# A two-layer graph attention kernel: head norms taken along rows with Newton steps on GpSimd, and a second layer norm taken by row chunks

## The reference

```python
# layer 0: 4 heads of 64
q, k, v = h @ Wq, h @ Wk, h @ Wv
attn = softmax(where(adj, q k^T * scale, -max));  out = (attn @ v) @ Wo + bo
# layer 1: 8 heads of 64
m = embs @ map_w.T + map_b
norm = max(||m_head||, 1e-8);  n = m_head / norm          # per node and head
cos_adj = (n n^T * ~mask > 0.1)
q, k = m @ q_w.T + q_b, m @ k_w.T + k_b
p = softmax(where(mask, -1e10, q k^T / 8)) * keep
adj_h = cos_adj * p
out = relu((adj_h @ sem_h) @ gcn_W.T / (adj_h.sum(-1) + 1))
```

## Time and profile before

| | us |
|---|---|
| median of 3 runs | 4123.62 |
| lowest, highest | 4120.02, 4124.43 |
| the profiled execution | 4121.26 |
| its span, first to last instruction | 4119.5 |
| TensorE busy | 3931.4 (95%) |
| TensorE weight loads busy | 3437.0 (83%) |
| VectorE busy | 2608.3 (63%) |
| ScalarE busy | 1979.3 (48%) |
| GpSimd busy | 1324.3 (32%) |

### The profile page before, as it was taken

One profiled execution on the slowest core, in us unless ns is written; L12 is line 12 of the kernel. 1 busy time (PEld: TensorE's weight loads), 2 busy tenths in 40 slices (PEclk: granted clock), 3 DMA queues, 4 the chain that ended last, 5 costly groups with the idle time before them and its releaser, 6 DMA issues.

```text
span 4119.5 us, 105002 instructions
## 1 busy us (share of the span) xinstructions
PE 3931.4 (95%) x32976; PEld 3437.0 (83%) x32976; DVE 2608.3 (63%) x9426; ACT 1979.3 (48%) x5583; POOL 1324.3 (32%) x2007
## 2 busy tenths in 40 slices
PE   7999999999999999999999999999999999999997
PEld 6888888888888888888888888888888888888886
DVE  4666666666666666666666666666666666666664
ACT  3554544544545445445454454454454544544544
POOL 3333333333332333333333333333333333333332
PEclk8999999999999999999999999999999999999998
DMA  3000000000000000000000000000000000000000
GB/s 87 16 32 26 22 32 16 32 32 16 32 27 21 32 18 30 32 16 32 29 18 32 22 25 32 16 32 32 16 32 27 21 32 16 32 32 16 32 27 17
DMA packets 65544, 111.77 MB, mean 27 GB/s; under 512 B 20880, under 2 KB 22448, under 8 KB 65520
## 3 DMA queue, kind: packets, MB, share of 16 engines
q1 hardware_dynamic: 64928, 110.12, 7.8%
q0 software_dynamic: 592, 1.35, 0.2%
HBM read 44.34 MB, written 33.55 MB: 19 GB/s over the span
## 4 chain that ended last, share of the span: by engine, by line
PE 65%; DVE 12%; issue 11%; ACT 6%; POOL 4%; DVEq 1%; DMA 1%; POOLq 0%; ACTq 0%; SPq 0%
PE bank L755 34%; PE bank L763 9%; PE bank L748 7%; PE bank L783 6%; PE bank L775 4%; ACT prob L501 3%; PE bank L883 3%; POOL prob L417 2%; DVE x_mid L663 2%; ACT att L475 2%; DVE prob L650 2%; DVE att L607 2%; DVE att L618 1%; POOL rstd L362 1%; DVE hT L640 1%
## 5 line engine op out<-in xcount | busy, mean ns | idle before, releaser
L475 ACT ACTIVATE att<-att,nmax 128x256 f32<-128x256 f32 x1024 | 509.7, 500 | 299.6 <-DVE nmax L607 299.6
L417 POOL TENSOR_SCALAR prob<-prob,rsum 128x256 f32<-128x256 f32 x512 | 241.1, 487 | 631.2 <-DVE rsum L657 628.2
L755 PE MATMUL bank<-hT,w_qkv 128*128 128x256 f32 x3072 | 414.9, 288 | 4.7 <-DVE hT L640 4.7
L755 PE MATMUL bank<-qkm,w_k 128*128 128x256 f32 x3072 | 416.6, 285 | 0.0
L755 PEld LDWEIGHTS bank<-hT,w_qkv 128*128 128x128 f32 x3072 | 376.9, 189 | 37.9 <-issue 24.2
L755 PE MATMUL bank<-hT,w_map 128*128 128x256 f32 x3072 | 396.7, 285 | 5.1 <-DVE hT L640 1.0
L618 DVE SCALAR_TENSOR_TENSOR att<-bank,att 128x256 f32<-128x256 f32 x1024 | 392.3, 420 | 4.0
L755 PE MATMUL bank<-qkm,w_q 128*128 128x256 f32 x3072 | 390.8, 283 | 0.0
L755 PEld LDWEIGHTS bank<-hT,w_map 128*128 128x128 f32 x3072 | 372.5, 189 | 18.4 <-DVE hT L640 17.3
L763 PE MATMUL bank<-w_v,hT 128*128 128x512 f32 x1536 | 385.3, 399 | 0.0
L755 PEld LDWEIGHTS bank<-qkm,w_k 128*128 128x128 f32 x3072 | 380.1, 188 | 5.0
(11 more groups left out here) (122 smaller groups left out, 7949.6 us busy)
## 6 DMA issues: line engine op xcount, KB each, us to landing
x_in<-x SPq DMA_DIRECT2D x64, 512.0 KB, 3.4
x_res<-x_mid SPq DMA_DIRECT2D x64, 512.0 KB, 3.1
out<-x_res SPq DMA_DIRECT2D x64, 512.0 KB, 2.8
adj<-adj SPq DMA_DIRECT2D x64, 64.0 KB, 2.6
att<-gcn_map POOLq DMA_DIRECT2D x2, 512.0 KB, 9.0
x_mid<-wq SPq DMA_DIRECT2D x1, 512.0 KB, 5.6
x_res<-wk SPq DMA_DIRECT2D x1, 512.0 KB, 6.8
v<-wv SPq DMA_DIRECT2D x1, 512.0 KB, 7.7
```

The costliest lines, as they stand in the source:

```text
L417: last = g.tensor_scalar(prob0[:, hd, c, :], prob0[:, hd, c, :], rsum0[:, hd, c:c + 1], 0.0, ALU.mult, ALU.add)
L475: s_.activation(e_sl, e_sl, ACT.Exp, bias=nmax1[:, p, c, e:e + 1], scale=-1.0, accum_out=esum1[:, p, c, e:e + 1]).then_inc(exp1_done, 1)
L755: last = t_.matmul(dst, w(ws, k)[:, t * 128:t * 128 + 128], rhs[:, rs, k, :], start=(k == 0 and i == 0), stop=(k == KT - 1 and i == 2))
```

## The change

Four things change together, and all five lists are new in order.

- Head norms as rows. GpSimd still squares `m32`. ScalarE rounds pairs of squares to fp32r (`sq0`, `sq1`) into the space of `nrm`, GpSimd subtracts to get the rest (`lo0`, `lo1`, 128x512 each). `ss` becomes 8 matmuls of 256 columns with a 0/1 selector `sel` as weights, whose output is already `[40, 256]`: rows 0 to 7 and again rows 32 to 39. The `rt` transposes on TensorE go.
- Inverse root by Newton steps. VectorE clamps and makes a first guess by an integer trick; GpSimd does three steps of four operations each on `[40, 256]`, each waiting for the one before; VectorE's `rt` then makes `rnT`.
- Layer norm by chunks. Each row chunk has its own aggregate, `rstd` and `norm`. `ht?a` and `ht?b` are now row chunks, and `qk*` and `m*` wait for `ht?b`.
- PSUM. `score` has banks 0 and 1 for itself and `cos` has 2 and 3, so both can be issued ahead of the turns. `turn_a`, `turn_b`, `value` and `back` share bank 4, one after the other. Products go round banks 5 to 7 (`PBANKS = 3`).

Its core (start-up code, waits in `SYNC`, and declarations are cut):

```diff
     TENSOR = [
-        "ht0a", ("score", 0), "ht0b", ("cos", 0), "qk0", "qk1", ("turn_a", 0), "qk2", ("turn_b", 0), "s0", "s1", ("value", 0),
-        "qk3", ("back", 0), ("score", 1), ("cos", 1), "s2", "s3", "pt0", "v0", "pt1", ("turn_a", 1), ("turn_b", 1), "pt2",
-        "pt3", ("value", 1), "av", ("back", 1), ("score", 2), ("cos", 2), "wo0", "wo1", ("turn_a", 2), ("turn_b", 2),
-        ("value", 2), ("score", 3), ("back", 2), "ht1a", "ht1b", ("cos", 3), "m0", "m1", "m2", ("turn_a", 3), ("turn_b", 3),
-        "m3", ("value", 3), "vv0", "ss", "q2", "q1", "q0", "k1", ("back", 3), "rt", "k0", "q3", "k3", "bc0", "bc1", "k2",
-        "vv1"
+        ("score", 0), "ht0a", "ht0b", ("cos", 0), ("score", 1), "qk0", "qk1", ("turn_a", 0), "qk2", ("turn_b", 0), "qk3",
+        ("value", 0), "s0", "s1", ("cos", 1), ("score", 2), "s2", "s3", ("back", 0), "v0", ("turn_a", 1), "pt0", "pt1",
+        ("turn_b", 1), "pt2", "pt3", ("value", 1), "av", ("back", 1), ("cos", 2), "wo0", "wo1", ("turn_a", 2), ("score", 3),
+        ("cos", 3), ("turn_b", 2), "ht1a", "ht1b", ("value", 2), "m0", ("back", 2), "m1", ("turn_a", 3), "m2", ("turn_b", 3),
+        "m3", ("value", 3), "vv0", "q1", "ss", "q2", "q0", "k0", "q3", "k2", ("back", 3), "k3", "vv1", "bc0", "k1", "bc1"
     ]
     SCALAR = [
...
+        ("exp_a", 1), ("exp_b", 1), ("unit", 1), ("value", 0), "exp0", "exp1", "exp2", "exp3", ("turn_a", 1), "pt0", "pt1",
+        ("turn_b", 1), "pt2", "pt3", ("exp_a", 2), ("value", 1), ("exp_b", 2), "av", ("turn_a", 2), ("turn_b", 2), "ht1a",
+        "ht1b", ("value", 2), ("exp_a", 3), "m0", ("exp_b", 3), "m1", ("turn_a", 3), "m2", ("turn_b", 3), "sq0", "m3", "sq1",
+        "q1", "q2", "q0", ("value", 3), "k0", "q3", "k3", "k2", "k1"
     VECTOR = [
...
+        "wo0", "wo1", "norm1a", "norm1b", ("score_a", 3), "ht1a", "ht1b", ("score_b", 3), ("cos_a", 3), ("factor", 2),
+        ("back", 2), ("cos_b", 3), "m0", "m1", "m2", "m3", "stats0", "vv0", "norm0", "q1", "ss", ("factor", 3), "q2", "q0",
+        "k0", "q3", "rt", "k2", "k3", ("back", 3), "vv1", "bc0", "bc1", "k1"
     POOL = [
-        ("unit", 0), "mid", "mask0", "sum0", "sum1", ("unit", 1), ("back", 0), "sum2", "sum3", "rstd1", ("back", 1),
-        ("back", 2), "m0", "rstd0", "m1", "m2", "m3", "pow", "mask1", ("back", 3)
+        ("unit", 0), "mask0", "mid", ("unit", 1), "sum0", ("back", 0), "sum1", "sum2", "sum3", ("back", 1), "rstd1a", "rstd1b",
+        "m0", "m1", "lo0", "m2", ("back", 2), "m3", "lo1", "rstd0", "root0", "root1", "root2", ("back", 3), "mask1"
     ]
-    PBANKS = 4
+    PBANKS = 3
...
+                    elif kind in ("root0", "root1", "root2"):
+                        k = 4 * (ROOT_STEPS * n + int(kind[4]))
+                        if kind == "root0":
+                            pool.wait_ge(guessed, n + 1)
...
+                        g.tensor_tensor(root_t, root_x, root_y, ALU.mult).then_inc(root_steps, 1)
+                        pool.wait_ge(root_steps, k + 1)
+                        pool.sem_inc(passed_gpsimd, 1)
+                        g.tensor_tensor(root_t, root_t, root_y, ALU.mult).then_inc(root_steps, 1)
+                        pool.wait_ge(root_steps, k + 2)
+                        pool.sem_inc(passed_gpsimd, 1)
+                        g.tensor_scalar(root_t, root_t, -0.5, 1.5, ALU.mult, ALU.add).then_inc(root_steps, 1)
+                        pool.wait_ge(root_steps, k + 3)
+                        pool.sem_inc(passed_gpsimd, 1)
+                        g.tensor_tensor(root_y, root_y, root_t, ALU.mult).then_inc(root_steps, 1)
...
                     elif kind == "ss":
-                        pe.wait_ge(msq_done, KT * n + KT)
+                        pe.wait_ge(sq_high_done, 2 * n + 2)
+                        pe.wait_ge(sq_low_done, 2 * n + 2)
                         empty(n, kind)
                         for t in range(KT):
-                            for c in range(C):
-                                last = t_.matmul(full[:, c * H1 + 2 * t:c * H1 + 2 * t + 2], msq[:, t, c * 128:c * 128 + 128], half_of[:, :], start=True, stop=True)
-                        last.then_inc(product_full, 1)
-                    elif kind == "rt":
-                        pe.wait_ge(rn_done, n + 1)
-                        empty(n, kind)
-                        for c in range(C):
-                            last = t_.transpose(full[0:H1, c * 128:c * 128 + 128], rn[:, c * H1:c * H1 + H1], ident[:, :])
+                            for i, part in enumerate((sq_high, sq_low)):
+                                last = t_.matmul(full[:, 0:N], sel[:, t, :], part[:, t, :], start=(t == 0 and i == 0), stop=(t == KT - 1 and i == 1))
                         last.then_inc(product_full, 1)
```

More of the change, by code:

```diff
@@ L19 @@
 COS_THRESHOLD = 0.1
+ROOT_GUESS = 1597463007.0
+ROOT_STEPS = 3
 MASKED_L1 = -1e10
@@ L61, in gnn_two_layers @@
-        ("turn_a", 1), ("turn_b", 1), "pt2", "pt3", ("value", 1), "av", ("exp_a", 2), ("exp_b", 2), ("turn_a", 2),
-        ("turn_b", 2), ("value", 2), "ht1a", "ht1b", ("exp_a", 3), "m0", ("exp_b", 3), "m1", ("turn_a", 3), "m2",
-        ("turn_b", 3), "m3", "q2", ("value", 3), "q1", "k1", "q0", "k0", "q3", "k3", "k2"
+        ("unit", 0), "ht0a", "ht0b", ("exp_a", 0), ("exp_b", 0), "qk0", "qk1", ("turn_a", 0), "qk2", ("turn_b", 0), "qk3",
+        ("exp_a", 1), ("exp_b", 1), ("unit", 1), ("value", 0), "exp0", "exp1", "exp2", "exp3", ("turn_a", 1), "pt0", "pt1",
@@ L192, in gnn_two_layers @@
         pick_made = count("pick_made")
+        sel_made = count("sel_made")
         fold_full = count("fold_full")
@@ L353, in _, with rstd_of @@
             pool.sem_inc(nlow_done, 2)
-            def rstd_of(k):
-                pool.wait_ge(stat_done, 4 * k + 4)
+            def rstd_of(k, c):
+                pool.wait_ge(stat_done, 4 * k + 2 * c + 2)
                 pool.sem_inc(passed_gpsimd, 1)
-                g.tensor_scalar(var_e[:, :], mv[:, :, 1], 1.0, LN_EPS, ALU.mult, ALU.add).then_inc(var_done, 1)
-                pool.wait_ge(var_done, 2 * k + 1)
+                g.tensor_scalar(var_e[:, c:c + 1], mv[:, c, 1:2], 1.0, LN_EPS, ALU.mult, ALU.add).then_inc(var_done, 1)
+                pool.wait_ge(var_done, 4 * k + 2 * c + 1)
                 pool.sem_inc(passed_gpsimd, 1)
-                g.tensor_tensor(rstd[:, :], var_e[:, :], minus_half[:, 0:C], ALU.pow).then_inc(var_done, 1)
-            pool.wait_ge(made, 9)
-            rstd_of(0)
+                g.tensor_tensor(rstd[:, c:c + 1], var_e[:, c:c + 1], minus_half[:, c:c + 1], ALU.pow).then_inc(var_done, 1)
+            pool.wait_ge(made, 15)
+            for c in range(C):
+                rstd_of(0, c)
             with nc.allow_non_contiguous_dma("small biases, once"):
@@ L672, in body @@
                                                 ALU.add, ALU.subtract).then_inc(product_done, 1)
-                    elif kind == "norm1":
-                        normalise(2 * n + 1, x_mid)
+                    elif kind in ("norm1a", "norm1b"):
+                        normalise(2 * n + 1, x_mid, "ab".index(kind[5]))
                     elif kind == "norm0":
-                        normalise(2 * n + 2, x_in)
+                        for c in range(C):
+                            normalise(2 * n + 2, x_in, c)
                     elif kind == "stats0":
                         dve.wait_ge(x_loaded, 16 * n + 32)
-                        row_stats(x_in, 0)
-                        row_stats(x_in, 1)
-                        mean_var(2 * n + 2)
+                        for c in range(C):
+                            row_stats(2 * n + 2, x_in, c)
                     elif kind in ("vv0", "vv1"):
@@ L822, in body @@
                     elif kind[:2] == "ht":
-                        t = 2 * "ab".index(kind[3])
-                        pe.wait_ge(h_ready, 4 * n + (2 if kind[2] == "0" else 4))
+                        c = "ab".index(kind[3])
+                        pe.wait_ge(h_ready, 4 * n + (1 if kind[2] == "0" else 3) + c)
                         empty(n, kind)
-                        transposes(full, lambda k, c: h[:, c, (t + k) * 128:(t + k + 1) * 128]).then_inc(product_full, 1)
+                        transposes(full, lambda k, half: h[:, c, (2 * k + half) * 128:(2 * k + half) * 128 + 128]).then_inc(product_full, 1)
                     elif kind[:2] == "qk":
@@ L829, in body @@
                         empty(n, kind)
-                        for chunks in (range(2), range(2, 4)):
-                            pe.wait_ge(product_done, out_of_psum(n, "ht0a" if chunks[0] == 0 else "ht0b"))
-                            last = project(full[:, 0:N], lambda s2, k: w_qkv[:, s2, w, k, :], t, hT, chunks)
-                        last.then_inc(product_full, 1)
+                        pe.wait_ge(product_done, out_of_psum(n, "ht0b"))
+                        project(full[:, 0:N], lambda s2, k: w_qkv[:, s2, w, k, :], t, hT).then_inc(product_full, 1)
                     elif kind == "v0":
@@ L864, in body @@
```

(6 more changed lines are left out.)

136 lines of the change are left out of this document (79 added, 57 removed), and 3 rows, old and new, of the table VECTOR.

## The result

The changed kernel takes 4222.6 us (4219.98 to 4223.51), the kernel before on the same chip 4124.0: 1.024 times as long, 95% interval 1.0222 to 1.0257. It is slower by 98.6 us, where +17 was forecast.

A forecast was written before the change was run, and what follows sets the result against it. TensorE, busy 95% of the span, was taken as the bound: its work plus holes. Terms summed to +0.32 us a round, times 63 +20, with the ends +17, added to 4123.6: 4141 us, range 4044 to 4200.

The forecast's parts named there:

- Work saved on TensorE: TensorE's work: `ss` as 8 matmuls and no `rt` transposes, -0.87 us a round.
- Second layer norm: TensorE's holes from `wo1` to `m0` shrink to 1.58 us from 2.75: -1.17 us a round.
- `pt3`: TensorE's hole at `pt3`, a wait for GpSimd's scaled `prob`, shrinks to 0.15 us: -0.18 a round.
- `q0`: TensorE waits at `q0` for the bank of `q1`, drained late behind `norm0`: +0.67 us a round.
- `bc0`: TensorE waits at `bc0` for the Newton chain, `rt` and the drain of `k2`: +0.72 us a round.
- Newton is longer: Rival on the GpSimd chain: a multiplication costs 0.74 us, the chain grows by 0.9, all uncovered: 4198 us, chance 0.17.
- Newton fits: Rival: holes at `q0`, `bc0` and `k1` (1.54 us) go in part or whole: 4044 to 4086 us, chance 0.33.
- `k1`: TensorE waits at `k1` for the bank of `k3`, which VectorE drains after `k2`: +0.15 us a round.
- `cos` 0: TensorE waits at `cos` 0 for `unit` 0, by way of ScalarE and GpSimd: +0.40 us a round.
- `wo0`: TensorE waits at the output projection, ScalarE's copy of `av` standing behind `exp_b` 2: +0.60 us a round.
- The ends: Outside the repeated rounds: start-up fills +2 us, first round +1, last round about -6.
- Rival B: Rival from the follow-ups: three product banks instead of four, and shared bank 4, hold TensorE up everywhere; two steps about 4205 us.

The follow-up runs named there:

- the run with four moves: Changed kernel with `norm0` behind `ss`, `rt` behind `k2` and `k3`, `av` ahead of `exp_b` 2, `score_a` 3 behind `ht1b`: 4087.6 us.
- two moves in one list: Changed kernel with, in VectorE's list, `norm0` behind `ss` and `rt` behind `k2` and `k3` but ahead of `back` 3: 4088.8 us, 0.9915 of before.

## Why the prediction was wrong, point by point

The measured 4222.6 lies above the range, which ended at 4200. The direction was the likeliest one, the size six times too small: 98.6 us for 17, from +1.41 a round instead of +0.32, and 18 us of a lower clock that had no term.

- **Work saved on TensorE** (-0.87): right. `ss` 0.94 instead of 0.97, and `rt` gone: -0.90.
- **Second layer norm** (-1.17): right in kind, too large. `m0` started 9.36 us behind `wo0`, where the walk gave 9.0 and the kernel before 10.18 (its 10.46 less the 0.28 that the walk leaves for `back` 2): -0.82. The time was lost on VectorE ahead of `ht1b`: its two aggregates wait for their statistics, for which the walk had no term, and the second ends at 5.32 on the round's clock instead of 4.9. From `ht1b` to `m0` it took 2.07, as walked (2.1). The hole ahead of `m0` was put on the mask ahead of `ht1a`; the run with four moves shows it is ScalarE's copy. The two aggregates, timeline of VectorE:

```profile
2068.28 0.18 DVE L574 BATCH_NORM_AGGREGATE mv<-stats 128x2 f32<-128x6 f32 x1 [0.15 <-DVE stats L571]
2070.05 0.18 DVE L574 BATCH_NORM_AGGREGATE mv<-stats 128x2 f32<-128x6 f32 x1 [0.15 <-DVE stats L571]
```

- **`pt3`** (-0.18): wrong, 0.38 before and after the change, now at `pt1`: 0.
- **`q0`** (+0.67): 0.38. Right place and releaser, shown by the run with `norm0` late.
- **`bc0`** (+0.72): 1.94. This is the term that failed, and all parts of it the same way. Newton's last operation ended at 35.03 of the round's clock instead of 34.4: 0.63, though the first started as walked (25.17 for 25.2). The multiplications took 0.73, not 0.64, nine times, +0.81, the scale-and-add 0.40, not 0.49, three times, -0.27, and the eleven hand-overs 0.1 more in all. I had bounded a multiplication by 0.62 and 0.74 and chosen half of a 512-wide operation. The error is in the halving: from 0.73 for 256 and 1.288 for 512 elements an operation costs 0.17 us once and 2.18 ns an element (an estimate from two points), and half of the long one drops half of the fixed part. The row of the same size and two different inputs, L410 with 738 ns, was right to 0.01 us; the 0.62 is of one tensor with itself. Then `rt` and the drain took 1.46 instead of 1.1 (0.28, 0.15 between, 0.41 and a drain of 0.48), and TensorE was ready at 34.55, not 34.8. 0.63 + 0.36 + 0.25 is 1.24, the size of the miss.
- The rival "Newton is longer" had just this price, 0.74, and this place, and gave 4198, still 24 us short. With 0.17 it was weighed too low: the chain had no slack, so each bound of its unknown cost was as near as the value I took. The rival "Newton fits", 4044 to 4086, is what the run with two steps shows, at 4062.4.
- **`k1`** (+0.15): 0.14. **`cos` 0** (+0.40): about 0.4, released by GpSimd's `nrm`, as forecast. **`wo0`** (+0.60): 0.3, and not by `exp_b` 2.
- Together the measured terms give +1.44, for 1.41 of the rounds. Without `bc0` the others miss by +0.35, +0.18, -0.29 and -0.30 and nearly cancel, which is luck.
- **The lower clock**: no case of the prediction had it. The first and last slices of the profile before showed it only where TensorE idles for long, and an idle time of 1.35 in each round was harmless there. Idle times of 1.8 and more weren't always, and the layer norm alone shows that none of that length is needed. It is 18 of the 98.6 us; with four steps each round has it.
- **The ends**: forecast -3, measured about -2 (4.2 + 1.9 - 8.3).
- What I hadn't seen at all is that the order of two names in VectorE's list could be worth 0.7 us through GpSimd's timing.

The Trainium skill's page GPSIMD Engine Reference, section 3.1, states about 2.6 cycles an element for two inputs, plus a dispatch that it does not put in figures for GpSimd; the slope of 2.18 ns found here is 2.6 cycles of the 1.2 GHz that its section 1 gives, so the trace agrees. Read for an estimate of the unknown duration, that form (a fixed part and a slope) would have kept me from halving. Its section 4.1, VectorE for elementwise work, is half right here: the chain is shorter there (about 2.0 us a step from its first start to its last end, its operations 0.41, 0.42, 0.29 and 0.42, against 3.15 on GpSimd), and its cost comes back as late drains.

Shown by runs: that the chain's length, `norm0` ahead of it and the drain of `k2` behind it each cost what they cost, and that rows hardly do. Rival B is out as the main cause, since the run with two steps has three product banks too. Argued only: that the layer norm's gain of 0.8 in the changed kernel needs the new order; the part alone doesn't have it, but no run put the new order on the old norm. Not tested: what a fourth product bank would give the new lists. Open: which rounds get the lower clock.

## What to carry to other kernels

When a change puts a chain of dependent small operations between two products, measure it against the work that lies between them in the fixed order, and price each operation by a row of the same size and the same number of inputs, never by half of a larger one. Then look at what stands ahead of its first and behind its last operation in each in-order list: here two moves in one list were worth 134 us, more than the whole loss. And a wait that grows past what the kernel has had so far can cost more than its length: here TensorE came back at half its clock in some rounds, with four steps in all, so a forecast needs a case for it.

## What the runs showed of the hardware

- VectorE's copy of 40x256 within SBUF takes 0.285 us by itself, 0.796 when it starts just behind the start of a two-input addition of 0.72 us on GpSimd, and 0.696 beside a one-input product of 0.61; it ends 0.14 to 0.15 us behind the GpSimd instruction in both cases. Where the copy started first, it took 0.275 (one case). Its 8x256 subtraction takes 0.415 by itself and 0.606 beside the product `mask1`. By one exchange in one list this undid a gain of 0.6 us a round. The Trainium skill (Advanced Engine Details and Errata, section Mode Summary) says that VectorE's second SBUF port is shared with GpSimd, and that GpSimd's instructions and those of VectorE in a two-port mode interfere with or block each other. For the copy the trace agrees, though no run shows in which mode it ran; on the subtraction, which has two inputs, that sentence does not bear.
- TensorE's granted clock fell to the lower level (0.56 over 3.2 us) behind an idle time of about 1.8 us in 12 of 61 rounds and not in the others, and behind one near 5 us in all 61 (0.50 to 0.56). How often does not follow the length alone: with 128 rows, 1.8 us, it was 6 of 61, and with `rt` behind `back` 3, 2.04 us, it was 7. Single idle times up to 1.36 us brought no slow round in the kernel before, nor 1.32 with `rt` between the drains; but with the layer norm alone 5 of 61 were slow, with no idle time above 0.9 in the round.
- GpSimd's 256-element multiplication is 0.730 us on 40 partitions and 0.737 on 128.
